# First MoE layer: from scattering rows into expert slots to storing them in token order and letting each expert gather them

## The reference

```
x = x + 0.5 * ffn(layernorm(x))
x = x + attn(layernorm(x))        # projections, softplus, cumulative sum over the sequence
x = x + 0.5 * ffn(layernorm(x))

ffn(x): 32 experts, capacity C = ceil(1.25 * 16384 / 32) = 640
  logits = xt @ w_router;  top1 = argmax;  gate = softmax value of top1
  pos  = running count of tokens that chose the same expert, in token order
  slot = top1 * C + pos if pos < C, else dropped
  buf[slot] = xt                          # 20,480 slots, some of them empty
  y = (silu(buf @ w_gate[e]) * (buf @ w_up[e])) @ w_down[e]
  out = xt + (y[slot] * gate, or 0 where dropped)
```

## Time and profile before

| | us |
|---|---|
| median of 3 runs (1722.61 to 1725.13) | 1724.47 |
| the profiled execution | 1724.29 |
| its span | 1722.5 |
| route (to the first instruction of the experts) | 298.5 |
| first experts, to the last result scatter issued | to 712.4 |
| attention with the second router | to about 1310 |
| second experts | to the end |

### The profile page before, as it was taken

How to read it: one execution, slowest core, us unless ns; L and a number is a source line. 1 busy time by engine, 2 the same in 40 slices (tenths; PEclk the granted TensorE clock), 3 DMA queues, 4 the chain that set the end, 5 groups by cost and what they waited for, 6 DMA issues and landing times. The chain is left out here.

```text
span 1722.5 us, 32675 instructions
## 1 busy us (share of the span) xinstructions
PE 1465.6 (85%) x10850; PEld 1416.1 (82%) x10850; DVE 1145.1 (66%) x2961; ACT 1103.7 (64%) x2324; POOL 861.4 (50%) x1149
## 2 busy tenths in 40 slices
PE   4766760899999999389999999999925999999997
PEld 4655650899999999389999999999925999999996
DVE  3534530677777777367778878877824777777775
ACT  4656760666666666268777777777714666666664
POOL 3277776244443434234346667666772343434343
PEclk9656655899999999799999999999967999999999
DMA  9996542666666667320122222211113444444541
GB/s 363 379 307 214 190 160 93 201 225 215 197 225 222 203 209 241 117 67 27 60 86 62 90 82 68 82 63 41 63 45 119 121 119 136 140 136 118 151 135 34
DMA packets 196854, 250.09 MB, mean 145 GB/s; under 512 B 24618, under 2 KB 181976, under 8 KB 192592
## 3 DMA queue, kind: packets, MB, share of 16 engines
q1 hardware_dynamic: 169040, 204.23, 37.3%
q0 software_dynamic: 27648, 43.78, 7.3%
HBM read 128.05 MB, written 152.17 MB: 163 GB/s over the span
## 5 line engine op out<-in xcount | busy, mean ns | idle before, releaser
L800 PE MATMUL ps<-xs,ws 128*128 128x320 f32 x3072 | 464.4, 310 | 0.0
L800 PEld LDWEIGHTS ps<-xs,ws 128*128 128x128 f32 x3072 | 454.7, 189 | 0.6 <-issue 0.6
L280 POOL DMA_INDIRECT slots<-xn,r x256 | 258.6, 1010 | 107.4 <-issue 97.5
L800 PE MATMUL ps<-ws,hs 128*128 128x256 f32 x1920 | 275.3, 291 | 28.1 <-DVE hs L721 28.1
L631 POOL DMA_INDIRECT x_rows<-ys,oidx x160 | 169.0, 1056 | 250.2 <-DVE ys L742 220.3
L631 POOL DMA_INDIRECT out<-ys,oidx x160 | 168.5, 1053 | 249.6 <-DVE ys L742 219.8
L800 PEld LDWEIGHTS ps<-ws,hs 128*128 128x128 f32 x1920 | 241.0, 190 | 41.1 <-DVE hs L721 41.1
L757 DVE TENSOR_TENSOR hf<-ps,sg 128x320 f32<-128x320 f32 x256 | 125.7, 491 | 164.1 <-ACT sg L685 164.0
L654 ACT CAST xs<-ps 128x512 fp32r<-128x512 f32 (+1 forms) x192 | 99.6, 520 | 160.0 <-PE ps L793 160.0
L707 DVE TENSOR_TENSOR ws<-wraw,ws 128x512 fp32r<-128x512 f32 x192 | 132.6, 692 | 82.6 <-ACT ws L647 79.5
L301 ACT ACTIVATE xn<-x,r 128x256 f32<-128x256 f32 x256 | 138.8, 591 | 66.2 <-DMA slots<-xn,r 37.4
(11 more groups left out here) (108 smaller groups left out, 2632.7 us busy)
## 6 DMA issues: line engine op xcount, KB each, us to landing
slots<-zero SPq DMA_DIRECT2D x32, 1300.0 KB, 10.2
xg<-slots SPq DMA_DIRECT2D x64, 650.0 KB
x<-in_x SPq DMA_DIRECT2D x32, 512.0 KB, 6.0
x_rows<-x SPq DMA_DIRECT2D x32, 512.0 KB, 3.6
wraw<-in_w_gate SPq DMA_DIRECT2D x64, 256.0 KB, 2.8
wraw<-in_w_up SPq DMA_DIRECT2D x64, 256.0 KB, 3.2
wraw<-in_w_down SPq DMA_DIRECT2D x64, 256.0 KB, 3.8
x<-x_rows SPq DMA_DIRECT2D x32, 512.0 KB, 5.2
```

The costliest lines, as they stand in the source:

```text
L280: nc.gpsimd.indirect_dma_start(out=self.slots, out_offset=bass.IndirectOffsetOnAxis(ap=self.slot[:, t % XR, k:k + 1], axis=0), in_=self.xn ...
L800: ins = pe.matmul(dst, left(a, k), right(b, k), start=(n == 0), stop=(n == len(terms) - 1))
```

## The change

In the first ffn only (the second keeps its scatter and its zero filled slots):

- `route` neither fills nor scatters. The rows `xn` of a batch go to a tensor `xn_rows` in token order, by one plain transfer of 2.1 MB from SyncE (`sp_rows`).
- The table slot -> token (`INV`, 128 x 160: position in the tile, and 160 tiles of slots) is made by 0/1 products. For each batch VectorE compares every token's slot, split into its low 7 bits and the rest, with 0..127 and 0..159 (`dve_hot`: 128 x 2048 and 128 x 2560 elements, bf16), and multiplies the second table by the tile number + 1 and by the lane. TensorE sums the products of both tables over all tokens in one PSUM bank (`pe_invert`, 32 matmuls of 128 x 160 a batch). After the last batch five small VectorE instructions make token numbers of it, with a number out of range where a slot is empty (`dve_inverse`).
- The residual moves from ScalarE to GpSimd (`pool_base`, 128 instructions of 128 x 256).
- The lags grow: `post` at S = 8t + 12, 13, 14 and 17, the count at + 15, `dve_hot` and `sp_rows` at + 18, `pe_invert` at + 20. The small statistics buffers get a third copy, and `pool_rstd` waits for the batch before the last.
- In the first experts GpSimd gathers the 640 rows of an expert by five indirect transfers, two experts ahead, in the same queue as the result scatters: gather(e + 2), scatter(e). Empty slots are skipped by the bounds check; `XG` is zeroed once at the start. The result scatter takes its indices from `INV`, and `out_index` goes.

```diff
@@ Tail
+            def sp_rows(self, sp, t):
+                rows = xn_rows.rearrange("(t j p) d -> t p j d", p=P, j=TB)
+                sp.wait_ge(self.ready.sem, self.ready.at(t + 1))
+                sp.dma_start(rows[t], self.xn[:, t % XR]).then_inc(self.scattered[t % XR], 16)
+            def dve_hot(self, dve, t):
+                dve.wait_ge(self.post_links.sem, self.post_links.n)
+                dve.wait_ge(self.matched.sem, self.matched.at(t + 1))
+                if t:
+                    dve.wait_ge(self.inverted.sem, self.inverted.at(t))
+                dve.tensor_tensor(self.hot_s[:], self.each_s[:], mid(self.lanes[:, 1, :], E * ET),
+                                  ALU.is_equal).then_inc(self.matched.sem, 1)
+                dve.tensor_tensor(self.hot_p[:], self.each_p[:], mid(self.lanes[:, 0, :], P), ALU.is_equal)
+                dve.wait_ge(self.matched.sem, self.matched.at(t + 2))
+                dve.tensor_tensor(self.hot_v[:, 0], self.hot_s[:], mid(TILE[:, TB * t:TB * t + TB], E * ET), ALU.mult)
+                dve.tensor_scalar(self.hot_v[:, 1], self.hot_s[:], LANE, None, ALU.mult).then_inc(self.hot.sem, 1)
+            def pe_invert(self, pe, t):
+                pe.wait_ge(self.hot.sem, self.hot.at(t + 1))
+                for j in range(TB):
+                    for v in range(2):
+                        ins = pe.matmul(ps[:, 6, E * ET * v:E * ET * v + E * ET], self.hot_p[:, :, j],
+                                        self.hot_v[:, v, :, j], start=(t == 0 and j == 0 and v == 0),
+                                        stop=(t == BATCH - 1 and j == TB - 1 and v == 1), skip_group_check=True)
+                ins.then_inc(self.inverted.sem, 1)
@@ post, step 3, first layer
+                        dve.tensor_copy(self.bits[:, 0, :], t1).then_inc(links.sem, 1)
+                        dve.tensor_scalar(self.bits[:, 1, :], self.bits[:, 0, :], P - 1, None, ALU.bitwise_and)
+                        dve.tensor_scalar(self.bits[:, 2, :], self.bits[:, 0, :], 7, None,
+                                          ALU.logical_shift_right).then_inc(links.sem, 1)
+                        dve.tensor_copy(self.lanes[:, 0, :], self.bits[:, 1, :])
+                        dve.tensor_copy(self.lanes[:, 1, :], self.bits[:, 2, :]).then_inc(links.sem, 1)
@@ route
-                LEAD, POST, SCATTER, BASE = 4, 9, 13, 3
+                LEAD, POST, COUNT, INVERT, BASE = 4, (12, 13, 14, 17), 15, 20, 3
-                    sp.wait_ge(zeroed, 1)
-                    for n in range(NFILL):
-                        fill(sp, 0, slots1, n)
...
+                    for S in range(NU + POST[3] + 2):
+                        if S % 2 == 1 and S // 2 < NQ4:
+                            q = S // 2
+                            stream.store(sp, q, tail.based)
+                            if q >= 1 and q - 1 + 4 * XR < NQ4:
+                                stream.load(sp, q - 1 + 4 * XR)
+                        for t in batches(S, POST[3] + 1):
+                            tail.sp_rows(sp, t)
@@ experts, GpSimd
+                    def gather(e):
+                        if e >= GR:
+                            pool.wait_ge(turned.sem, turned.at(NQ * (e - GR + 1)))
+                            pool.wait_ge(based.sem, based.at(e - GR + 1))
+                            pool.wait_ge(ysum.sem, ysum.at(NQ * (e - GR + 1)))
+                        apart(pool)
+                        for k in range(ET):
+                            nc.gpsimd.indirect_dma_start(
+                                out=XG[:, e % GR, k, :], out_offset=None, in_=xn_rows,
+                                in_offset=bass.IndirectOffsetOnAxis(ap=INV[:, ET * e + k:ET * e + k + 1], axis=0),
+                                bounds_check=T - 1, oob_is_err=False,
+                            ).then_inc(xg_gathered[e % GR], 16)
+                    if turn == 0:
+                        gather(0)
+                        gather(1)
                     for e in range(first, end):
+                        if turn == 0 and e + 2 < end:
+                            gather(e + 2)
                         scatter(e)
```

More of the change, by code:

```diff
@@ L40 @@
 XR = 3
+GR, YR = 3, 3
 NQ4 = NT // 4
@@ L112, in macaron @@
         zeroed = sem("zeroed")
-        filled = [sem(f"filled{k}") for k in range(2)]
+        filled = sem("filled")
+        INV = sb([P, E * ET], U32, name="inv")
+        XG = sb([P, GR, ET, RW], F32, name="xg")
         IDENT = CF[:, 0:128]
@@ L205, in __init__ @@
                 self.carried = count(f"{tag}_carried")
-                self.ready = count(f"{tag}_slots", 2)
+                self.ready = count(f"{tag}_slots", 3)
                 self.total = sem(f"{tag}_total")
-                self.scattered = [sem(f"{tag}_scattered{k}") for k in range(XR)]
+                self.out = 16 * (TB if slots is not None else 1)
+                self.scattered = [sem(f"{tag}_rows_out{k}") for k in range(XR)]
+                if slots is None:
+                    self.lanes = s([P, 2, TB], BF16)
+                    self.bits = s([P, 3, TB], U32)
+                    self.each_p = s([P, P, TB], BF16)
+                    self.each_s = s([P, E * ET, TB], BF16)
+                    self.hot_p = s([P, P, TB], BF16)
+                    self.hot_s = s([P, E * ET, TB], BF16)
+                    self.hot_v = s([P, 2, E * ET, TB], BF16)
+                    self.hot = count(f"{tag}_hot")
+                    self.matched = count(f"{tag}_matched")
+                    self.inverted = count(f"{tag}_inverted")
+                    self.invf = s([P, 3, E * ET])
                 self.pool_links = Links(sem(f"{tag}_pool"))
@@ L464, in _ @@
                         stream.load(sp, q)
-                    sp.wait_ge(zeroed, 1)
-                    for n in range(NFILL):
-                        fill(sp, 0, slots1, n)
[L468 to L473, removed]
+                    for q in range(8, 4 * XR):
+                        stream.load(sp, q)
+                    for S in range(NU + POST[3] + 2):
[6 more added lines that the diff above has]
+                            tail.sp_rows(sp, t)
                     stream.all_stored(sp)
+                    tail.all_rows(sp)
                 @block.gpsimd
@@ L494, in _ @@
                     tail.act_setup(act)
-                    tail.based.grant(act)
-                    for S in range(NU + 12):
-                        for t in batches(S, POST + 2):
+                    for S in range(NU + POST[1] + 2):
+                        for t in batches(S, POST[1] + 1):
                             tail.act_exp(act, t)
@@ L539, in _ @@
                     tail.pe_setup(pe)
-                    for S in range(NU + 12):
+                    for S in range(NU + INVERT + 1):
                         if S == 4:
@@ L547, in _ @@
                             ins.then_inc(s_prep, 1)
-                        for t in batches(S, POST + 2):
+                        for t in batches(S, COUNT):
                             tail.pe_count(pe, t)
@@ L575, in macaron, with rows_in, experts @@
         ysum = count("e_ysum", 2)
-        def experts(turn, slots, rows):
+        def rows_in(eng, e):
+            if e < E:
+                eng.wait_ge(xg_gathered[e % GR], 16 * ET * (e // GR + 1))
+            else:
+                eng.wait_ge(xg_in[(e - E) % GR], 16 * ((e - E) // GR + 1))
+        def experts(turn, rows):
             with ExitStack() as st:
@@ L1218, in macaron @@
         route()
-        experts(0, slots1, x1_rows)
+        experts(0, x1_rows)
         attention()
-        experts(1, slots2, out)
+        experts(1, out)
 _ARRAYS = ["x", "w_proj0", "w_delta_t", "w_c", "w_c_t", "w_r_t", "a_vec", "b_vec", "d_vec", "b_delta",
```

161 lines of the change are left out of this document (93 added, 68 removed).

## The result

The changed kernel takes 1745.37 us (median of 4 runs, 1744.70 to 1746.30) where the kernel before takes 1723.54 beside it: ratio 1.0127, 95% interval 1.0109 to 1.0144. The forecast was 1714 and faster. The time lies inside the range, at its upper end, where rival C stood; the mechanism is nearest to rival E's, a long inversion, which was priced at 1726.

A forecast was written before the change was run, and what follows sets the result against it. Route was taken as bound by the fill, then GpSimd's scatter issue; the first experts by TensorE. 1724.3 - 52 (route) + 4.7 (first gathers) + 38.7 (GpSimd's issues) = 1715.7, put at 1714; range 1676 to 1746.

The forecast's parts named there:

- rival C: Route, VectorE: products run one element a step, 10.4 us a batch, 28 us a batch in all; 1744 us, chance 0.14.
- rival E: Route, TensorE: stride makes the inversion 7.3 us or more, some +12, 1726 us; sign: inversion over 7 us; chance 0.09.
- I take 5, since weights and columns of these rows overlap: Route, TensorE: the inversion's price in us a batch, chosen between 4.5 by columns and 7 with a stride factor.
- the chain: Route: engines waiting on each other from known slots to those two batches later, 51.2 us for two batches.
- The count of columns: Route, TensorE: the inversion priced by 32 matmuls of 160 columns, 4.5 us.
- The row store as the new wait: Route: ScalarE waits for the rows' store, landing in 8 us; about 25 us a batch, experts start at 246.
- The start of the chain: Route: first batch's slots known at 65 us, conversions and products 6.1 later.
- VectorE's products, two elements at a time: Route, VectorE: all four wide products at two elements at a time, 5.4 us a batch.
- GpSimd's ten issues: First experts: five scatters and five gathers an expert take 13.9 us on GpSimd against 12.42, +38.7 us.
- Rival D: First experts, GpSimd: every issue pays the contended price, 14.35 us an expert, +52; 1729 us, chance 0.10.
- rival B: Route runs at VectorE's sum, -72, and gathers cost 13.2 us an expert, +18; 1675 us, chance 0.22.
- The dropped `out_index` "covered anyway": First experts, VectorE: dropping its two instructions of 0.16 us gains nothing, being covered anyway.

The follow-up runs named there:

- experiment 6: Its last kernel: changed kernel with moving tables (hot_v) side by side and rows stored two steps earlier; 1704.73 us, ratio 0.9887 to the kernel before.
- experiment 2: Changed kernel with only the moving tables (hot_v) laid out side by side; one run, 1935.66 us, where the kernel before took 1815.
- experiment 1: Changed kernel with only the weights' table (hot_p) laid out side by side; one run, 1971.10 us, where the kernel before took 1815.
- experiment 3: Changed kernel with both tables side by side, made by 48 small VectorE instructions a batch; median 1957.45 us, where the kernel before took 1815.
- experiments 2 and 4: Changed kernel with moving tables side by side: 1935.66 us, again 1945.99; the second also adds rows stored two steps earlier: 1930.86, beside 1814.24 for the kernel before.
- experiment 5: Changed kernel whose first experts load 640 consecutive rows by one plain transfer each instead of gathers; 1705.85 us, ratio 0.9896 to the kernel before.

## Why the prediction was wrong

The step that failed: "I take 5, since weights and columns of these rows overlap", the price of the inversion, which measured 9.7, and with it the chain in which it stood: TensorE and not the row store's round trip set the pace of route.

- **Inversion: 5 us forecast, 9.7 measured.** The count of columns was right for columns that lie side by side: 4.5 forecast, 4.49 measured at a granted clock of 0.50 (at 100.32 us of the last kernel of experiment 6). The stride costs a factor of 2.1 there, and more where the clock is up (the short inversion takes down to 3.6 in experiment 2), and not the 1.1 that I let it have. I had a strided row with a factor of 1.47, made 7 of it (4.5 x 1.47 is 6.6), and then discounted that for an overlap of weights and columns which no row of a strided matmul showed. The overlap wasn't the matter: with the weights side by side the inversion still takes 9.41 (experiment 1). The Trainium skill (SBUF — State Buffer, Door 1) says that each access that crosses to a new 16-byte line pays, and I named it as evidence against this layout; the trace agrees for the moving operand, 0.30 us for 160 columns against 0.11 to 0.14, and doesn't for the weights, where experiment 1 shows 0.3 us an inversion and experiment 3 none.
- **Rival E, as priced, was wrong too.** It let the stride count "once in each pair of batches, twice at the end" and made +12 of 2.3 us. With 9.7 it counts in each batch. The inversions of the changed kernel begin at 73.11 and 276.63: 203.5 / 7 = 29.1 us a batch, where the forecast has 231.5 + 6.1 - 71.1 = 166.5, 23.8 a batch. The difference is 5.3, about the size of the inversion's 4.7. The forecast never set TensorE's whole batch beside its chain: with its own terms that is 8 x 2.0 + 5 + 3.4 = 24.4 us, just under the 25.6 of the chain, and with the measured inversion 29.1. So nearly every microsecond of the inversion lengthens the batch, and TensorE is busy for 36 to 39 of 40 us. That step is an estimate; the experiments give the share: columns 25 us, with 2.7 us a batch more VectorE work in the same edit, so 25 is more likely too little than too much.
- **The row store as the new wait.** The forecast's main chain was wrong for this kernel and right one step further on: a wait of 23.3 us in 4 with the long inversion, 41 in 5 with the short one, and 15 us of route when the store goes out two steps earlier. A row store landed in 10.4 us by the median, not 8. With the price right and the chain as I had it, route would have ended at 262 to 264 (experiments 2 and 4), not at 246; so some 17 of the 43 us belong to that chain's terms and to the slower products of those experiments, which no run separates.
- **The start of the chain** held: first inversion at 73.11 against 65 + 6.1 = 71.1.
- **VectorE's products, two elements at a time:** 5.4 forecast, 1.50 + 1.24 + 1.48 + 0.96 = 5.2 measured. The first three bear that out; the last, with one input, is faster than two at a time. Rival C is refuted for the layout that the kernel has.
- **GpSimd's ten issues:** mechanism right, 13.9 forecast and 13.65 measured; every gather takes at least 0.994 us, the contended ones up to 1.51. Rival D (14.35) isn't met, nor rival B, in which TensorE doesn't wait for gathers. TensorE reaches its first transposes 8.3 us after the first gather (297.42 - 289.16) where it took 4.2: +4.1 for +4.7. But the stage grew by 31.2 and not by 43.4. Cadence makes 29 x 0.25 = 7.3 of the difference. Another 2.5 is a double count: the first scatter starts 26.4 us after the first gather against 24.2 before, +2.2, and I had added the whole 4.7 in front of GpSimd's queue. Some 2 us are left unassigned.
- **The dropped `out_index` "covered anyway":** it wasn't. It was 0.25 us an expert on the path to TensorE, seen at 12.17 against 12.42 once the gathers are out of the way (experiment 5). In the changed kernel itself GpSimd sets the cadence over the whole stage, so the gain is swallowed.

The two errors, +43 and -12, had opposite signs, and their sum, +31, put the time at the place of rival C (1744) by a mechanism that isn't C's. The figure agrees by luck, the reason doesn't. E had the cause, and its sign, an inversion of over 7 us, is what the trace shows, but with the smallest chance and a price that was too low.

## What to carry to other kernels

When data is laid out for the engine that writes it, price the layout for every engine that reads it. Here a table with the tile index innermost saves VectorE 2.7 us a batch and costs TensorE 5.5 (77.5 against 33.7 us in 8 batches). An engine that looks idle in one stretch of the trace of before (17.5 of 40 us) can be the bound after 9.7 us a batch are added: read it where it is fullest, here 32 of 40. If a batch's order is written by hand, add up each engine's whole batch, and do it at the upper end of each uncertain price too: with mine, 8 x 2.45 + 7 + 3.4 = 30 us, TensorE would have been the bound, above the forecast's chain of 25. And a stage that gets free time by moving work into a queue of another stage must be priced there: the gathers cost 38 of the 53 us that route gives in the last kernel of experiment 6.

## What the runs showed of the hardware that was not expected

- **A moving operand with a step of 32 bytes costs the same at both clocks.** Windows of the changed kernel over two inversions, then over two parts of the second (columns as in the windows above):

```profile
109.04:118.51 9.47, 9.47 (x34) 4.82 (x35) 4.20 (x19) 0.78 (x2) 8.92 (x20) 0.50 0.74 217
136.37:145.90 9.53, 9.53 (x32) 4.87 (x33) 9.23 (x32) 1.71 (x4) 4.10 (x9) 0.64 0.01 2
137.00:142.00 5.00, 5.00 (x18) 2.52 (x17) 4.83 (x19) 0.36 (x1) 0.58 (x2) 0.71 0.02 3
142.00:146.00 4.00, 4.00 (x15) 2.08 (x14) 3.90 (x14) 1.27 (x3) 3.62 (x8) 0.50 0.00 0
```

  At a granted clock of 0.50 and of 0.64 it is 9.64 and 9.71 us, with the DMA engines busy (0.74) or idle (0.01). The second begins at 2.4 GHz (granted clock 1.00 until 138) and falls to 1.2 within it: 18 matmuls in 5.00 us at 0.71 and 15 in 4.00 at 0.50 are 0.28 and 0.27 us each in these counts, where a few records can be missing. So its pace, 1.9 ns a column by the whole inversions, doesn't follow the clock. That the read of the operand sets it is likely and not shown.
- **It doesn't bring TensorE's clock up, though the engine is busy throughout.** The units behind it take 2.4 us (118.51 to 120.90), the price of 1.2 GHz, behind all six inversions that have units behind them. Behind the contiguous inversion of the kernel of experiment 6 they take 1.25 (133.58 to 134.83), that of 2.4 GHz, in four of six cases; in the other two TensorE had idled for about 4 us before the inversion, and the clock rises within the unit behind it. That kernel's mean granted clock from 80 to 120 us is 0.76 against 0.54. So the long inversion costs more than its own length; how much of the 25 us this is, no run separates.
- **The change's price depends on a condition of the chip whose cause isn't known:** the ratio of the same two kernels was 1.013 on some runs and 1.088 (1.0847 to 1.092) on others, with the loss in the experts. Without gathers it was 0.9896 in both. The row store lands in 10.4 and 10.6 us by the median, and GpSimd's instruction for a gather takes 1.01 and 1.00; how long a gather takes to land the traces don't give. The cause stays open.
